# Step 0 of a conv-attention kernel: sums, differences and low parts change hands between GpSimd and VectorE, and the four queues are written in a new order

## The reference

```
x = x + conv_block(layernorm_over_channels(x, eps=1e-6))
    # conv_block(u): h = group_norm(u, 32 groups, eps=1e-5) * gamma + beta
    #                qkv = conv1d(h, qkv_w (768,256,16)) + qkv_b     16 taps, same padding
    #                per head (4 heads of 64): softmax(q k / 8) v
    #                u + conv1d(heads, proj_w (256,256,5)) + proj_b
t = tokens(x)
t = t + ffn(layernorm(t, eps=1e-5))   # reads one-hot fields of 16, shifts a byte, adds 2 at two digits
```

## Time and profile before

| what | us |
|---|---|
| three runs | 1025.39, 1027.53, 1027.74 (median 1027.53) |
| the profiled execution, its own time | 1025.49 |
| its span, first to last instruction | 1023.7 |
| TensorE busy | 922.5 (90%) |
| VectorE busy | 732.6 (72%) |
| ScalarE busy | 665.5 (65%) |
| GpSimd busy | 349.2 (34%) |
| mean granted TensorE clock | 0.976 |

### The profile page before, as it was taken

One profiled execution on the slowest core, in us unless ns is written; L12 is line 12 of the kernel. 1 busy time (PEld: TensorE's weight loads), 2 busy tenths in 40 slices (PEclk: granted clock), 3 DMA queues, 4 the chain that ended last, 5 costly groups with the idle time before them and its releaser, 6 DMA issues.

```text
span 1023.7 us, 19614 instructions
## 1 busy us (share of the span) xinstructions
PE 922.5 (90%) x7826; PEld 738.7 (72%) x7826; DVE 732.6 (72%) x1234; ACT 665.5 (65%) x1112; POOL 349.2 (34%) x225
## 2 busy tenths in 40 slices
PE   2578799998999999999999999999999989897774
PEld 1466678786878878777768878877887768786663
DVE  6989959664767677787776656465647665877867
ACT  5757557773787478677875757466657665576621
POOL 2688834331540255265421210121102114313420
PEclk9999899999999999999999999999999989999977
DMA  8050245987897746475546544645648662343322
GB/s 293 1 218 22 88 148 130 185 176 199 179 221 197 190 106 147 109 213 133 120 84 175 135 95 108 145 111 104 125 124 172 176 161 64 98 120 83 104 62 83
DMA packets 291866, 138.32 MB, mean 135 GB/s; under 512 B 269120, under 2 KB 271552, under 8 KB 291264
## 3 DMA queue, kind: packets, MB, share of 16 engines
q1 hardware_dynamic: 291776, 137.08, 54.3%
HBM read 48.80 MB, written 16.95 MB: 64 GB/s over the span
## 4 chain that ended last, share of the span: by engine, by line
PE 46%; DVE 21%; ACT 13%; issue 7%; DMA 3%; SPq 1%; POOL 1%; ACTq 0%; POOLq 0%; DVEq 0%
PE cM L1235 11%; PE cQ L1235 10%; PE cP L1235 10%; ACT arena L1111 5%; DVE W L1518 4%; PE psS L1372 3%; PE psT L1372 3%; DVE smx L1713 3%; PE psV L1349 3%; DVE arena L1690 3%; DMA arena<-arena 2%; PE psV L1353 2%; PE cM L1190 1%; ACT arena L916 1%; DVE arena L1564 1%
## 5 line engine op out<-in xcount | busy, mean ns | idle before, releaser
L1235 PE MATMUL cM<-U,W 128*128 128x256 f16 x1728 | 209.7, 279 | 29.9 <-DVE U L1526 18.3
L1235 PEld LDWEIGHTS cM<-U,W 128*128 128x128 f16 x1728 | 171.7, 100 | 65.9 <-DVE U L1526 18.5
L1235 PE MATMUL cQ<-U,W 128*128 128x256 f16 x1728 | 202.8, 273 | 3.9 <-POOL U L647 2.1
L1235 PE MATMUL cP<-U,W 128*128 128x256 f16 x1728 | 201.1, 273 | 2.7 <-ACT y_all L971 1.6
L1235 PEld LDWEIGHTS cQ<-U,W 128*128 128x128 f16 x1728 | 168.0, 98 | 35.1 <-POOL U L647 2.4
L1235 PEld LDWEIGHTS cP<-U,W 128*128 128x128 f16 x1728 | 168.5, 98 | 32.3 <-ACT y_all L971 1.9
L1690 DVE SCALAR_TENSOR_TENSOR arena<-arena,smx 128x1024 f16<-128x1024 f32 x128 | 176.5, 1379 | 12.7 <-ACT arena L1121 12.2
L726 POOL TENSOR_TENSOR ap<-ap 128x512 f32<-128x512 f32 x24 | 40.9, 1703 | 361.8 <-ACT ap L983 361.6
L1121 ACT ACTIVATE arena<-arena,smx 128x1024 f16<-128x1024 f32 x128 | 147.3, 1150 | 4.3
L1713 DVE TENSOR_REDUCE smx<-psS 128x1 f32<-128x1024 f32 x64 | 78.1, 1220 | 67.4 <-PE psS L1372 67.0
L1104 ACT ACTIVATE smx<-smx,tiny 128x1 f32<-128x1 f32 x128 | 37.5, 293 | 126.9 <-DVE smx L1713 126.5
(11 more groups left out here) (220 smaller groups left out, 1316.4 us busy)
## 6 DMA issues: line engine op xcount, KB each, us to landing
U<-kept_u SPq DMA_DIRECT2D x21, 520.0 KB, 5.6
staging<-w_qkv SPq DMA_DIRECT2D x20, 512.0 KB, 5.9
wsum<-w_qkv SPq DMA_DIRECT2D x24, 256.0 KB, 4.1
U<-kept_u SPq DMA_DIRECT2D x7, 780.0 KB, 5.0
kept_u<-temp_b SPq DMA_DIRECT2D x9, 520.0 KB, 3.6
arena<-x_tok SPq DMA_DIRECT2D x8, 512.0 KB, 6.6
arena<-arena SPq DMA_DIRECT2D x16, 256.0 KB, 3.5
W<-x_tok SPq DMA_DIRECT2D x4, 1024.0 KB, 6.2
```

Of the source, the lines that this page charges most:

```text
L1235: last = mm(out, W[:, j, wl, c, QTAPS * (3 * family + third) + tap, :], u[:, ul, c, at + tap:at + tap + QUART], start=((g, c, t) in OPENER ...
```

## The change

Counted by calls in `first_step`, 27 pieces of work change their engine. To VectorE go 17 of GpSimd's 30 weight sums, five low parts of the input (0,4), (0,5), (1,1), (1,2), (1,5), and the fine differences (1,0); to GpSimd go the three fine differences of batch 0 and the differences (0,1). Because two engines now feed each counter, the functions wait on it in order. The order of all four compute queues in step 0 is new; SP issues `load_u(1, 0)` ahead of `store_u(1, 5)`. ScalarE's square roots read the variance itself and add epsilon as their bias, where VectorE wrote variance plus epsilon into a working tile first (it still writes it, for its Newton step, but nobody waits for that).

```diff
+        def rstd_early(ch, eng, var, sign, eps, cols, sq_done, runs):
+            lo, hi = cols
+            n, s, out = (early[:, r, lo:hi] for r in range(3))
+            ch.done(nc.vector.tensor_scalar(n, var, sign, eps, ALU.mult, ALU.add))
+            eng.wait_ge(S[sq_done], runs)
+            newton(ch, n, s, nt[:, 2, lo:hi], nt[:, 1, lo:hi], out)
...
+        def first_sum(eng, ops, m, h):
...
+            wait(eng, "wsum_done", SUMS * m + at)
...
@@ SyncE
-            copy_k(0, 0)
             store_u(1, 3)
             store_u(1, 4)
+            load_u(1, 0)
             store_u(1, 5)
-            for q in range(4):
-                load_u(1, q)
+            copy_k(0, 0)
+            load_u(1, 1)
...
@@ ScalarE
-            def ln_root(q):
-                sqrt("ln_var", "ln_sq", q + 1, early[:, :, 0:8])
             def ln_root(q):
+                act.wait_ge(S["pads"], 5)
+                act.wait_ge(S["ln_var"], 8 * (q + 1))
+                a(nt[:, 1, 0:8], ln[:, BATCH_AT[q], :, 1], ACT.Sqrt, bias=nt[:, 0, 8:9]).then_inc(S["ln_sq"], 1)
...
@@ GpSimd, first_step
+                first_sum(pool, g, 0, 0)
+                first_sum(pool, g, 0, 3)
+                fine_differences(pool, g, 0, 0)
+                first_sum(pool, g, 0, 5)
...
+                differences(pool, g, 1, 0)
+                differences(pool, g, 1, 1)
+                u_low(pool, g, 1, 0)
+                fine_differences(pool, g, 1, 1)
...
@@ TensorE, first_step, tile 1
                 conv_item(0, 0, 1, 0, 0, 1)
+                z_transpose(2)
                 conv_item(0, 0, 1, 0, 0, 2)
+                group_mean(2)
+                weight_top(2, psV[:, 2 * P:3 * P])
                 conv_item(0, 0, 1, 0, 1, 1)
...
@@ VectorE, first_step, around weight tile 1
+                w_lo(1, 1)
+                first_sum(dve, v, 1, 3)
+                w_lo(1, 4)
+                fine_differences(dve, v, 1, 0)
+                half_y(0, 0, 0, 1)
...
+                group_stats(2)
+                w_add(2)
+                first_sum(dve, v, 1, 5)
...
+                group_norm(2)
+                w_scale(2)
+                u_low(dve, v, 1, 1)
+                group_norm_end(2)
+                w_lo(1, 2)
```

More of the change, by code:

```diff
@@ L250, in pow2, with newton @@
             ch.step(v.tensor_scalar(inverse.bitcast(I32), bits[:, 0:1], 1.0, -k * EXP23, ALU.mult, ALU.add))
-        def rstd_ask(var, eps, work, asked, sign=1.0):
-            nc.vector.tensor_scalar(work[:, 0, :], var, sign, eps, ALU.mult, ALU.add).then_inc(S[asked], 1)
-        def rstd_end(ch, eng, out, work, q, sq_done, runs):
+        def newton(ch, n, s, q, rough, out):
             v = nc.vector
-            n, s = (work[:, r, :] for r in range(2))
-            eng.wait_ge(S[sq_done], runs)
-            ch.step(v.reciprocal(q, s))
+            ch.step(v.reciprocal(q, rough))
             ch.step(v.tensor_tensor(s, n, q, ALU.mult))
@@ L436, in fine_differences, with u_low, raw_pair @@
                                 ALU.subtract).then_inc(S["sub_done"], 1)
+        def u_low(eng, ops, b, part):
+            u = u_home(b, part)
+            if b >= 2:
+                u_high(eng, b, part)
+            eng.wait_ge(S["uhi_done"], u_place(b, part))
+            wait(eng, "ulo_done", u_place(b, part) - 1)
+            ops.tensor_tensor(u_part(u, part, 1), u_source(b, part), u_part(u, part, 0), ALU.subtract).then_inc(S["ulo_done"], 1)
+        def raw_pair(m, h):
+            stage = wst(m)
+            if h < 4:
+                c, t = h // 2, h % 2 * QTAPS
+                return stage[:, c, 0, t:t + QTAPS], stage[:, c, 1, t:t + QTAPS]
+            c, q = h % 2, (h - 6) // 2
+            return stage[:, c, q, 0:QTAPS], stage[:, c, q, QTAPS:PH_TAPS]
+        def first_sum(eng, ops, m, h):
+            order = sums_of(m)
+            at = order.index(h)
+            if at >= 4:
+                eng.wait_ge(S["wlo_done"], place(m, order[at - 4]))
+            elif m == 1 or (m == 2 and at < 2):
+                eng.wait_ge(S["wlo_done"], place(m - 1, sums_of(m - 1)[(8, 9, 6, 7)[at]]))
+            elif m == 2:
+                eng.wait_ge(S["wlo_done"], place(1, 10))
+            wait(eng, "wsum_done", SUMS * m + at)
+            weights_in(eng, m, part_of(h)[0])
+            if h in (4, 5):
+                pair = [sum_home(m, order.index(2 * (h - 4) + t)) for t in range(2)]
+            else:
+                pair = raw_pair(m, h)
+            ops.tensor_tensor(sum_home(m, at), pair[0], pair[1], ALU.add).then_inc(S["wsum_done"], 1)
         def home(k):
@@ L638, in _ @@
             g = nc.gpsimd
[L640 to L675, removed]
             def sums(m, i):
@@ L1401, in _ @@
             v = nc.vector
-            norm_chains = [Chain(dve, "c_a", q, 21) for q in range(NB)]
+            norm_chains = [Chain(dve, "c_a", q, 14) for q in range(NB)]
             def layer_stats(q):
@@ L1426, in layer_norm_end @@
                     .then_inc(S["z_nm"], 1)
-            group_chains = [Chain(dve, "c_g", b, 18) for b in range(NB)]
+            group_chains = [Chain(dve, "c_g", b, 17) for b in range(NB)]
             def group_stats(b):
@@ L1622, in last_stage @@
                 if kind == "norm":
-                    rstd_ask(stats[:, :, 1], 1e-5, nt[:, :, 0:count], "f_var")
-                    rstd_end(ch, dve, stats[:, :, 1], nt[:, :, 0:count], nt[:, 2, 0:count], "f_sq", run + 1)
+                    n, s, q = (nt[:, r, 0:count] for r in range(3))
+                    v.tensor_scalar(n, stats[:, :, 1], 1e-5, None, ALU.add).then_inc(S["f_var"], 1)
+                    dve.wait_ge(S["f_sq"], run + 1)
+                    newton(ch, n, s, q, s, stats[:, :, 1])
                     ch.step(v.scalar_tensor_tensor(nmr[:, b, i0:i0 + count], stats[:, :, 0], -1.0, stats[:, :, 1], ALU.mult,
```

315 lines of the change are left out of this document (149 added, 166 removed).

## The result

| what | before | after |
|---|---|---|
| median (lowest to highest) | 1026.64 (1024.96 to 1028.14), 9 runs | 1022.42 (1018.29 to 1023.52), 9 runs |
| profiled execution, its own time | 1025.49 | 1022.97 |
| its span | 1023.7 | 1021.1 |
| TensorE, VectorE, ScalarE, GpSimd busy | 922.5, 732.6, 665.5, 349.2 | 924.3, 732.7, 665.8, 313.3 |
| mean granted TensorE clock | 0.976 | 0.971 |

The ratio of times is 0.9949, 95% interval 0.9932 to 0.9966: faster by 0.5%. In a second group of runs it was 0.9961 (0.9946 to 0.9975). The medians are 4.2 apart, the two profiled spans 2.6.

What follows compares the result with a forecast made beforehand. VectorE, delayed by GpSimd in two-input SBUF work, was taken to bound step 0. +0.9 - 3.7 + 1.0 - 2.1 = -3.9 gave 1021.6 from the profile, 1023.6 from the median; the middle is 1022.6, range 1015 to 1031.

Steps and rivals of the forecast that it cites:

- The start: Start of step 0: the first square root's table load now follows its wait for the variance, +0.9 (0.7 to 1.3).
- The stretch: Step 0, VectorE's first low part to low part 9 of tile 2: 101.2 instead of 104.9, a gain of 3.7.
- The long stand-still: TensorE before low part 2 of tile 1: idle 11 to 14, then 3.4 more from the lower clock.
- The end of step 0: After low part 9: VectorE has 3.9 more work before low part 13, needed by item 17; +1.0 (0 to 3).
- The load of U: Step 1: TensorE's 2.14 wait goes because the load stands ahead of the store; -2.1 (0 to -2.1).
- The sum: Whole kernel: +0.9 - 3.7 + 1.0 - 2.1 = -3.9.
- (b): Rival: in step 0 less delay only pays for VectorE's 5.9 added work; 1025.5 to 1027, chance 0.20.
- (a): Rival: only the time both engines share counts; stretch 94.5 to 97, gain 8 to 10, time 1016.5, chance 0.20.
- (c): Rival: VectorE reaches low part 2 of tile 1 so late that TensorE ends step 0 later; 1032, chance 0.20.

Runs made afterwards that it cites:

- e1: Changed kernel with ScalarE's square-root table load moved ahead of its wait by a small root at the start; median 1020.34, ratio to before 0.9951.
- e6: Changed kernel with batch 0's three fine-difference pairs and its second difference back on VectorE; median 1028.57, ratio to before 1.0019.
- e4: Changed kernel with TensorE's weight top 1 behind its first item instead of its third; median 1018.83, ratio to before 0.9925.
- e5: Changed kernel with low parts 2 and 3 of tile 1 ahead of the third batch's group statistics, their TensorE items also earlier; median 1021.26, ratio to before 0.9953.
- e10: Changed kernel with low part 10 of tile 2 ahead of the low part of k on VectorE; median 1022.80, ratio to before 0.9965.
- e2: Kernel before, with only SP's first load of U for step 1 issued ahead of batch 1's last store; median 1022.85, ratio to before 0.9969.
- e3: Changed kernel with all 17 sums that had gone to VectorE back on GpSimd; median 1029.92, ratio to before 1.0041.
- e9: Changed kernel with early table load, early weight top 1, low part 10 first and two y scale chains moved on VectorE; median 1019.33, ratio to before 0.9935.

## Why the prediction was right, and where its steps were off

1022.6 was predicted and 1022.42 measured. The profile's own gain is 2.6 to the first trace; the prediction had 3.9. By its steps:

- **The start, +0.9**: measured +1.0, and e1 shows that it is the table load and that it reaches the end. The load ends at 9.27 and the root starts at 9.28, so no drain is seen at this load. The rule that the prediction cites from the Trainium skill (ScalarE: Activation LUTs, What ACT_TABLE_LOAD costs) would have made it 2.3 (an estimate); the measurement decides.
- **The stretch, -3.7**: measured -3.0, by two errors that cancel. The own work of VectorE came as counted, a sum at 0.60 for the 0.61 assumed, and e6 shows that it counts (4.6 more of it, 4.6 to 4.9 lost). The forecast was also 0.4 short of its own bill: 85.7, 13.9 lost to GpSimd and the 2 give 101.6, not 101.2. The delay by GpSimd was 10.7, not 14 plus 2. But VectorE was idle 5.5, of which I had no more than hops. The largest, 3.7, is the step that failed: the hand count let weight top 1 be served at once, while on TensorE it stands behind three items, and those run at the lower clock after the idle time of 11.15, 6.74 for 36 matmuls. In e4, with weight top 1 behind one item, VectorE's wait is 0.57 instead of 3.68, and step 0 ends 2.7 earlier.
- **The long stand-still**: 11 to 14 predicted from 69 to 84, low part 2 at 84.99, granted clock 0.50 in 79 to 91, 2.5 lost to the clock for 3.4 assumed. The 34 items behind it are right (sixteen of tile 1, where the text ahead of the prediction says fifteen, and 18 of tile 2). It was covered: e4 moved everything 2.7 forward with the stand-still unchanged, and filling it (e5) gained nothing.
- **The end of step 0, +1.0**: measured +1.5 (13.5 from low part 9 to `values` against 12.0), with the wrong reason. I named low part 13 and item 17. What limits is low part 10: it stands behind a low part of k and ends at 128.0, and the last eight items (10.7) follow it without a gap. e10 adds that ScalarE's copy is due within 0.7 of it.
- **The load of U, -2.1**: measured -2.3 by the length of step 1, in every kernel that has either of the two edits. The one term that was certain is nearly the whole gain of the profile.
- **The sum**: in the first trace +1.0 - 3.0 + 1.5 - 2.3 = -2.8, against 2.6 of the span. That the median nonetheless fell on 1022.4 is luck: the wait for the last transposition in step 2 is between 3.05 and 7.35 over 14 traces, and step 2 between 101.6 and 108.1. Whether the change shifts that wait on average is open. e2, whose step 0 is that of before, has a median 3.8 lower with a profile 2.3 lower, so a surplus like that of the changed kernel (4.2 against 2.6) comes without any move in step 0. By its ratio e2 gained 1.8 to 4.6, which holds the 2.3, so the surplus may be noise.

Of the rivals, (b) is nearer to the outcome than my forecast: in step 0 nothing but 0.1 to 0.9 net was won, and the load of U made the gain. Its reason is not what happened: for 5.9 of added work VectorE's delay fell by 11.8 (22.5 to 10.7). Of the 5.9 that this leaves, 2.9 went into more idle time, 1.0 into the start and 1.5 into the end of step 0. The shared bill (a) is refuted by e6. (c) had its stand-still, and not its price.

## What to carry to other kernels

When work moves between two engines that hinder each other, count the own work of the engine that sets the end in full, and expect relief from the other only where the two meet. For every wait of that engine, look at what stands ahead of the instruction it waits for, and at which clock: a transpose misplaced on TensorE, which is not the bound, cost 2.7. Compare two executions from an event that both reach ahead of the edit: from the start of the program e5 looked like a gain, from VectorE's last wait ahead of its edit it is a loss of 0.9. And read a small gain by stages of the trace before crediting it to the large edit; here one line in a DMA queue brought nearly all of it.

## What the runs showed of the hardware

- The same sum of two 128x512 f32 tiles takes 0.60 from start to start on VectorE (0.68 by itself) and 1.23 on GpSimd (1.27 by itself). A pair of fine differences on VectorE took 1.30 at its shortest (e6, at 57.69) and 3.48 (after) and 5.30 (e3) beside GpSimd's work.
- A square root of 128x8 took 0.30 on ScalarE with its bias and input read from SBUF, and 0.16 without a bias and with input and output in PSUM. The small root of e1, 128x1 in SBUF without a bias, took 0.20, so most of the difference goes with the bias.
- A table load in the program stood behind the wait for the data when its instruction had two waits, and ahead of it when it had one.
- TensorE's waits of 2.11 that were over at 103.97 (e4) and 101.24 (e9) were followed by 24 matmuls in 2.79 in one kernel (e4) and in 4.45 in another (e9), so the length of the last wait alone does not tell the granted clock behind it.
